# Gate and up of a feed-forward net: four sums of two products each in three shared PSUM banks, instead of two sums of five

## The chip, the cores and the metric

The kernel runs on one core of a Trainium2 chip. The metric is the device time of one execution in microseconds (us). A core has four engines that matter here: TensorE (PE in the profile; PEld are its weight loads), VectorE (DVE), ScalarE (ACT) and GpSimd (POOL). SyncE (SP) issues most DMAs. TensorE writes its results to PSUM, in banks of 512 float32 columns; VectorE and ScalarE read them from there.

## The reference

Four blocks run one after the other on x, 6250 rows of 512 numbers: a graph convolution, a feed-forward net with ternary weights, a second graph block, and a mixture of 16 experts. The change is in the feed-forward net, which the reference computes on the normalised rows:

```python
def _quantize_weight(w, group_size):            # group_size 128
    o, i = w.shape
    wg = w.reshape(o, i // group_size, group_size)
    scale = jnp.mean(jnp.abs(wg), axis=-1, keepdims=True) + EPS
    wq = jnp.clip(jnp.round(wg / scale), -1.0, 1.0) * scale
    return wq.reshape(o, i)
...
gate = _bitlinear(x, w_gate)                    # (6250, 512) by (1408, 512) transposed
up = _bitlinear(x, w_up)
h = jax.nn.silu(gate) * up
return _bitlinear(h, w_down)                    # back to 512
```

A quantised weight is -1, 0 or 1 times a scale, and there is one scale for each output feature and each block of 128 of the 512 inputs. So `gate` is a sum over four input blocks (DK = 4), each with its own scale.

## The kernel before

There are four stages, a to d. Stage a (to 168 us) makes tables for the graphs. Stage b (to about 560 us) gathers messages and prepares the weights of the feed-forward net in between. Stage c (to about 1,930 us) holds the feed-forward net, and around it the end of the first graph block and the row norms. Stage d does the rest.

**Stage b.** PE fetches table rows in 136 rounds of 20 small products (`products`, L1202 and L1205), which DVE picks out of PSUM (`pick`, L990). After every eighth round one block of 128 of the 1408 hidden features (f = 0 to 10) is prepared: ACT takes absolute values and signs, DVE quantises (`quantize`, `wide`), PE turns the blocks (`wide`, L1215 and L1216), ACT writes them to `wgu_hi`, and DVE writes a remainder to `wgu_lo` (`wide_rest`, L961). The four input blocks are taken in pairs. The even block of a pair is kept as -1, 0, 1; the odd one is multiplied by the ratio of the two scales (`wodd`, L952 to L954), so that a pair can be summed under one scale. Weights that carry this ratio are kept in a high part (`wgu_hi`) and a low part (`wgu_lo`).

**Stage c.** The 49 tiles of 128 rows are taken seven at a time, in a group of four (g = 0, 512 columns) and a group of three (g = 1, 384 columns); the seven rounds i = 0 to 6 are one unrolled, five passes of a loop, one unrolled. Each group has 11 steps, one for each f, so there are 154 steps. In a step PE does, in this order: `gate` (two sums of five products, into the banks pG0 and pG1), `up` (two sums of five, into pU0 and into pG0 again), and `down` of the step before (three products for each tile, 12 or 9, L1523). The five products of a sum are the even block's weights with the high and the low part of x, the odd block's with both, and the odd block's low part with the high part of x.

The sums leave PSUM as follows. ACT reads pG0 with the pair's scale into `gate_sum` (L1590). DVE reads pG1, scales it and adds it to `gate_sum` (L1722). ACT reads the second sum of up, which lies in pG0, into `up_sum` (L1596), and DVE adds pU0 to it (L1728). ACT makes silu of `gate_sum` in `sil` (L1599), DVE multiplies it by `up_sum` (L1732), ACT writes the high part to `hT` (L1603), DVE the low part (L1738), and `down` of the next step reads both.

**The order.** Each engine has its own queue and runs it in order. The order is written by hand in `groups`: after gate, up, low and down of each f, tables name what else is done there for the next group (`ahead`: building one-hot matrices with `build`, L173 to L1672; `sums`, L257 to L267; `layer1`, L1472, L1566 and L1680; statistics, norms, transposes) and for the last one (`behind`: residual L1744, statistics L1686, rows L1617, L1620 and L1759). This is called side work below. SP loads `wd` for each step, and POOL gathers messages (L132) beside all of it.

**Waits.** `wait_alone` makes an engine wait for a semaphore in an instruction of its own. PE may write a bank again once it has been read: gate's pG0 waits for `up_b` (ACT has read up's second sum), pG1 for `gate_b` (DVE has read it), pU0 for `up_a` (DVE), and up's pG0 for `gate_a` (ACT has read gate's first sum).

## Time and profile before

| what | value |
|---|---|
| median of 3 runs | 3246.15 us (3240.7 to 3249.64) |
| the profiled execution's own time | 3251.79 us |
| its span | 3250.0 us |
| busy in the span | PE 2693.1 us (83%), PEld 1942.7 (60%), DVE 1886.2 (58%), ACT 1259.4 (39%), POOL 1891.1 (58%) |
| mean granted clock of TensorE | 0.929 of full speed |
| steps of the feed-forward net | from 663.6 to about 1911 us |
| one pass of its loop (22 steps) | 182.34 us, from 1036.50 to 1218.84 |

The span is the time from the first to the last instruction of the profiled execution; 1.79 us of its own time lie around it. Busy shares are averages over stages with different limits, so the stages are read one by one. Durations of matmuls include their pipeline: the distance between the starts of two of them is less than the duration of one.

### The profile page before, as it was taken

The page shows a single profiled execution, that of the slowest core. Times are in us where ns is not written, and L with a number is a line of the kernel's source. Part 1 is how long each engine was busy: PE and PEld are TensorE (multiplying, and loading weights), DVE is VectorE, ACT ScalarE, POOL GpSimd, SP SyncE. Part 2 cuts the span into 40 slices and gives each one's busy share as a digit, 9 for nine tenths or more (in the row PEclk, how much of TensorE's full clock was granted, in tenths as well). Part 3 has the DMA queues.
Part 4 walks back from the last instruction along what each step waited for, and adds up shares of the span by engine and source line. Part 5 has one row for each costly group of instructions (what it writes and reads, how often), then busy time and mean ns, then how long its engine had stood idle before and what let it go on. Part 6 is the DMA issues. An engine that isn't in the chain of part 4 may idle for free. (4 is left out here: it accounts for less than half of the span.)

```text
span 3250.0 us, 59097 instructions
## 1 busy us (share of the span) xinstructions
PE 2693.1 (83%) x16318; PEld 1942.7 (60%) x16319; DVE 1886.2 (58%) x3394; ACT 1259.4 (39%) x2019; POOL 1891.1 (58%) x1940
## 2 busy tenths in 40 slices
PE   7789865579998989898999957778787887878799
PEld 7779864457777777777777743334343333435577
DVE  7679777646665565666666553333434444443687
ACT  2288643334544445444444440111222121214454
POOL 1077770577777777777400017777776767771465
PEclk9999985689999999999999978989999999998799
DMA  6354530213333333333323347777777877775574
GB/s 225 120 140 121 126 84 3 63 36 98 97 84 102 98 113 87 107 98 107 93 80 101 97 147 219 226 232 220 235 244 231 246 227 240 243 234 170 172 242 145
DMA packets 239794, 483.61 MB, mean 149 GB/s; under 512 B 75343, under 2 KB 92969, under 8 KB 239535
## 3 DMA queue, kind: packets, MB, share of 16 engines
q0 software_dynamic: 103936, 233.92, 26.6%
q1 hardware_dynamic: 135598, 246.49, 23.2%
q8 instruction: 132, 2.16, 0.3%
q14 instruction: 128, 1.04, 0.1%
HBM read 413.43 MB, written 73.35 MB: 150 GB/s over the span
## 5 line engine op out<-in xcount | busy, mean ns | idle before, releaser
L1975 POOL DMA_INDIRECT rows<-xn_rows,srcT x784 | 743.1, 948 | 273.0 <-issue 239.4
L132 POOL DMA_INDIRECT msg_c<-hid_rows,srcT x744 | 755.0, 1015 | 241.8 <-issue 225.7
L2114 PE MATMUL pV<-rows,oh 128*128 x2240 | 557.8, 398 | 145.0 <-DVE oh L2409 48.8
L1492 PE MATMUL gates<-xT,wgu_hi 128*128 128x384 f32 (+1 forms) x1848 | 481.5, 383 | 42.5 <-ACT gate_sum L1590 21.6
L2114 PEld LDWEIGHTS pV<-rows,oh 128*128 x2240 | 225.2, 101 | 463.4 <-issue 291.2
L1523 PE MATMUL accs<-wd,hT 128*128 128x512 f32 x1617 | 403.9, 397 | 15.9 <-DVE hT L1738 15.9
L1492 PEld LDWEIGHTS gates<-xT,wgu_hi 128*128 128x128 f32 x1848 | 343.1, 194 | 111.1 <-issue 65.8
L1523 PEld LDWEIGHTS accs<-wd,hT 128*128 128x128 f32 x1617 | 301.8, 188 | 87.7 <-issue 27.9
L2409 DVE SCALAR_TENSOR_TENSOR oh<-ids,bases,dstT 128x896 f32 x160 | 184.1, 1150 | 227.4 <-issue 164.0
L2397 DVE TENSOR_TENSOR agg<-agg,pV x161 | 110.1, 684 | 320.9 <-PE pV L2114 320.3
L132 POOL DMA_INDIRECT msg_b<-hid_rows,srcT x240 | 242.3, 1010 | 76.2 <-issue 72.0
L2246 ACT ACTIVATE between<-agg,invdeg 128x512 f32 (+1 forms) x49 | 35.3, 721 | 553.2 <-DVEq L121 553.2
L1205 PE MATMUL pG<-table,los 128*128 128x200 f16 x2176 | 247.5, 256 | 0.0
L1205 PEld LDWEIGHTS pG<-table,los 128*128 128x128 f16 x2176 | 200.6, 101 | 2.4
L2202 PE MATMUL pY<-weT,erT 128*128 128x512 f32 (+1 forms) x768 | 195.3, 404 | 3.8 <-DVE erT L2526 3.7
L2144 PE MATMUL pW<-wgT,aT 128*128 128x512 f32 x392 | 184.1, 614 | 15.0 <-DVEq L2432 14.9
L1958 POOL IOTA bases<- 128x49 f32 x1 | 0.2, 188 | 335.1 <-POOLq L390 335.1
L1596 ACT ACTIVATE up_sum<-gates,wscale 128x512 f32<-128x512 f32 (+1 forms) x154 | 97.6, 634 | 224.9 <-PE gates L1492 224.8
L1728 DVE SCALAR_TENSOR_TENSOR up_sum<-pU,wscale,up_sum 128x512 f32<-128x512 f32 (+1 forms) x154 | 105.0, 682 | 136.4 <-ACT up_sum L1596 132.2
L1492 PE MATMUL pU<-xT,wgu_hi 128*128 128x512 f32 (+1 forms) x616 | 168.1, 396 | 6.1 <-DVE up_sum L1728 6.1
L1492 PE MATMUL gates<-xT,wgu_lo 128*128 128x512 f32 (+1 forms) x462 | 172.3, 373 | 0.0
L1722 DVE SCALAR_TENSOR_TENSOR gate_sum<-gates,wscale,gate_sum 128x512 f32<-128x512 f32 (+1 forms) x154 | 105.3, 684 | 115.0 <-PE gates L1492 80.2
(426 smaller groups left out, 4525.0 us busy)
## 6 DMA issues: line engine op xcount, KB each, us to landing
wd<-wd_rows SPq DMA_DIRECT2D x154, 512.0 KB
lo<-lo_rows SPq DMA_DIRECT2D x68, 256.0 KB, 3.4
we<-in_L_ffn_expert_w SPq DMA_DIRECT2D x16, 1024.0 KB
x_rows<-xr SPq DMA_DIRECT2D x49, 256.0 KB, 4.3
xn_rows<-pair SPq DMA_DIRECT2D x49, 256.0 KB, 2.2
rows<-xn_rows,srcT POOLq DMA_INDIRECT x784
res<-x_rows SPq DMA_DIRECT2D x49, 256.0 KB, 3.9
x_rows<-agg SPq DMA_DIRECT2D x49, 256.0 KB, 4.1
```

The costliest lines, as they stand in the source:

```text
L132: nc.gpsimd.indirect_dma_start(msg[:, c, :], None, table, bass.IndirectOffsetOnAxis(ap=srcT[:, c:c + 1], axis=0)).then_inc(landed[u % 2], 16)
L1205: last = nc.tensor.matmul(into, los[:, g // 2 % LP, b, at:at + P], table1[:, j, b].rearrange("p f h -> p (f h)"), start=False, stop=(b == ...
L1492: last = nc.tensor.matmul(ps[:, 0:n], w, v, start=(m == 0), stop=(m == len(terms) - 1))
L1523: last = nc.tensor.matmul(acc4[j][:], h, wd[:, slot, w, :], start=(f == 0 and m == 0), stop=(f == FB - 1 and m == 2))
L1722: nc.vector.scalar_tensor_tensor(gate_sum[:, 0:n], pG[1][:, 0:n], wscale[:, f, 1:2], gate_sum[:, 0:n], ALU.mult, ALU.add).then_inc(s["gate ...
L1728: nc.vector.scalar_tensor_tensor(up_sum[:, 0:n], pU[0][:, 0:n], wscale[:, FB + f, 0:1], up_sum[:, 0:n], ALU.mult, ALU.add).then_inc(s["up_ ...
L1975: nc.gpsimd.indirect_dma_start(rows[:, u % RING, c, :], None, xn2_rows, bass.IndirectOffsetOnAxis(ap=srcT[:, u * Q + c:u * Q + c + 1], axi ...
L2114: last = nc.tensor.matmul(pV[:, ds(to, 1), :].rearrange("p a d -> p (a d)"), oh[:, ds(to, 1), c, :].rearrange("p a d -> p (a d)"), rows[:, ...
L2144: nc.tensor.matmul(pW[:], aT[:, k % 2, c, :], wgT[:, c, :], start=(c == 0), stop=False)
L2202: last = nc.tensor.matmul(pY[f % 2][0:n, :], erT[:, f % 2, j, c, 0:n], weT[:, e % 2, k, c, :], start=(j, k, c) == terms[0], stop=(j, k, c) ...
L2397: nc.vector.tensor_tensor(at, at, pV[:, ds((v + 1) % 2, 1), :].rearrange("p a b -> p (a b)"), ALU.add).then_inc(s["added"], 1)
L2409: nc.vector.scalar_tensor_tensor(oh[:, ds(v % 2, 1)].rearrange("p a q n -> p (a q) n"), bc(ids.unsqueeze(1), (P, Q, P)), bases[:, ds(tile, ...
```

## The change

A sum now takes one input block alone: its two products are the block's weights (-1, 0, 1) with the high and the low part of x. Gate has four such sums and so has up, in three banks that are used in a ring: gate's go to pG0, pG1, pU0, pG0, up's to pG1, pU0, pG0, pG1. ACT still reads the first sum of each, and DVE the other three, each scaled and added to `gate_sum` or `up_sum`, one after the other. `wgu_lo`, `wodd` and the work that made them are gone; `wscale` holds four scales for each feature, not two. The silu on ACT now waits for the third of DVE's sums, and PE's waits on a bank follow the ring.

```diff
-        wgu_lo = sb(ffn, "wgu_lo", [P, 2 * FB, DK // 2, P], F32R)
-        wscale = sb(ffn, "wscale", [P, 2 * FB, DK // 2], F32)
+        wscale = sb(ffn, "wscale", [P, 2 * FB, SP], F32)
...
-                    even, odd = (sc[:, 1, 0:2 * DK].rearrange("p (e b) -> p e b", b=2)[:, :, b] for b in range(2))
-                    ratio = sc[:, 3, 0:DK]
-                    nc.vector.tensor_copy(wscale[:].rearrange("p (k f) e -> p k f e", k=2)[:, :, f, :], even.rearrange("p (k e) -> p k e", k=2))
-                    own.step(nc.vector.reciprocal(ratio, even))
-                    own.step(nc.vector.tensor_mul(ratio, odd, ratio))
-                    nc.vector.tensor_tensor(wodd[:], wthree[:].rearrange("p (e b) c -> p e b c", b=2)[:, :, 1, :],
-                                            bc(ratio.unsqueeze(2), (P, DK, P)), ALU.mult).then_inc(s["wq"], 1)
+                    scales = sc[:, 1, 0:2 * DK].rearrange("p (k e) -> p k e", k=2)
+                    nc.vector.tensor_copy(wscale[:].rearrange("p (k f) e -> p k f e", k=2)[:, :, f, :], scales).then_inc(s["wq"], 1)
...
-                def wide_rest(f):
-                    dve.wait_ge(s["hi"], f + 1)
...
                     for j in range(2):
-                        for e in range(DK // 2):
-                            nc.tensor.matmul(pW[:, j, 2 * e, :], wthree[:, j * DK + 2 * e, :], identb[:], start=True, stop=True)
-                            last = nc.tensor.transpose(pW[:, j, 2 * e + 1, :], wodd[:, j * DK // 2 + e, :], ident[:])
+                        for e in range(SP):
+                            last = nc.tensor.matmul(pW[:, j, e, :], wthree[:, j * DK + e, :], identb[:], start=True, stop=True)
...
-            pU = [pb(ctx, "pU0", [P, 4 * P], F32), pG[0]]
+            pU = [pb(ctx, "pU0", [P, 4 * P], F32)]
+            ring = [pG[0], pG[1], pU[0]]
+            gate_at = [ring[e % 3] for e in range(SP)]
+            up_at = [ring[(SP + e) % 3] for e in range(SP)]
...
                 def hidden(ps, g, f, which, e):
-                    hi, lo = wgu_hi[:, which * FB + f], wgu_lo[:, which * FB + f]
+                    hi = wgu_hi[:, which * FB + f]
                     x_hi, x_lo = xT[g][:, 0], xT[g][:, 1]
                     n = len(GROUPS[g]) * P
-                    a, b = 2 * e, 2 * e + 1
-                    terms = ((hi[:, a, :], x_hi[:, a, :]), (hi[:, a, :], x_lo[:, a, :]), (hi[:, b, :], x_hi[:, b, :]),
-                             (hi[:, b, :], x_lo[:, b, :]), (lo[:, e, :], x_hi[:, b, :]))
+                    terms = [(hi[:, e, :], x_hi[:, e, :]), (hi[:, e, :], x_lo[:, e, :])]
...
-                    wait_alone(pe, s["up_b"], step + 1, s["fence_pe"])
-                    hidden(pG[0], g, f, 0, 0).then_inc(s["gate_ps"], 1)
-                    wait_alone(pe, s["gate_b"], step + 1, s["fence_pe"])
-                    hidden(pG[1], g, f, 0, 1).then_inc(s["gate_ps"], 1)
+                    wait_alone(pe, s["up_b"], 3 * step + 2, s["fence_pe"])
+                    hidden(gate_at[0], g, f, 0, 0).then_inc(s["gate_ps"], 1)
+                    wait_alone(pe, s["up_b"], 3 * step + 3, s["fence_pe"])
+                    hidden(gate_at[1], g, f, 0, 1).then_inc(s["gate_ps"], 1)
+                    hidden(gate_at[2], g, f, 0, 2).then_inc(s["gate_ps"], 1)
+                    wait_alone(pe, s["gate_a"], step + 1, s["fence_pe"])
+                    hidden(gate_at[3], g, f, 0, 3).then_inc(s["gate_ps"], 1)
 
                 def up(i, g, f):
                     step = steps_before(i, g, f)
-                    wait_alone(pe, s["up_a"], step + 1, s["fence_pe"])
-                    hidden(pU[0], g, f, 1, 0).then_inc(s["up_ps"], 1)
-                    wait_alone(pe, s["gate_a"], step + 1, s["fence_pe"])
-                    hidden(pU[1], g, f, 1, 1).then_inc(s["up_ps"], 1)
+                    wait_alone(pe, s["gate_b"], 3 * step + 1, s["fence_pe"])
+                    hidden(up_at[0], g, f, 1, 0).then_inc(s["up_ps"], 1)
+                    wait_alone(pe, s["gate_b"], 3 * step + 2, s["fence_pe"])
+                    hidden(up_at[1], g, f, 1, 1).then_inc(s["up_ps"], 1)
+                    wait_alone(pe, s["gate_b"], 3 * step + 3, s["fence_pe"])
+                    hidden(up_at[2], g, f, 1, 2).then_inc(s["up_ps"], 1)
+                    wait_alone(pe, s["up_a"], step + 2, s["fence_pe"])
+                    hidden(up_at[3], g, f, 1, 3).then_inc(s["up_ps"], 1)
...
-                    dve.wait_ge(s["gate_ps"], 2 * step + 2)
                     dve.wait_ge(s["gate_a"], step + 1)
-                    nc.vector.scalar_tensor_tensor(gate_sum[:, 0:n], pG[1][:, 0:n], wscale[:, f, 1:2], gate_sum[:, 0:n],
-                                                   ALU.mult, ALU.add).then_inc(s["gate_b"], 1)
+                    for e in range(1, SP):
+                        dve.wait_ge(s["gate_ps"], SP * step + (e + 1))
+                        if e > 1:
+                            dve.wait_ge(s["gate_b"], (SP - 1) * step + (e - 1))
+                        nc.vector.scalar_tensor_tensor(gate_sum[:, 0:n], gate_at[e][:, 0:n], wscale[:, f, e:e + 1], gate_sum[:, 0:n],
+                                                       ALU.mult, ALU.add).then_inc(s["gate_b"], 1)
```

`up` on DVE is changed as `gate` is, with `up_ps`, `up_b` and `up_at`; ACT's two reads take `gate_at[0]` and `up_at[0]`.

On PE, the rows of the step f = 1 of the first group of four tiles, before (gates holds two banks, pU is the third; x4 is four products in a row):

```order
L1492 MATMUL gates<-xT,wgu_hi 128x512 x4
L1492 MATMUL gates<-xT,wgu_lo 128x512
L1492 MATMUL gates<-xT,wgu_hi 128x512 x4
L1492 MATMUL gates<-xT,wgu_lo 128x512
L1492 MATMUL pU<-xT,wgu_hi 128x512 x4
L1492 MATMUL pU<-xT,wgu_lo 128x512
L1492 MATMUL gates<-xT,wgu_hi 128x512 x4
L1492 MATMUL gates<-xT,wgu_lo 128x512
L1523 MATMUL accs<-wd,hT 128x512 x12
```

and the same step in the changed kernel (line 1492 has become 1478, line 1523 has become 1516):

```order
L1478 MATMUL gates<-xT,wgu_hi 128x512 x4
L1478 MATMUL pU<-xT,wgu_hi 128x512 x2
L1478 MATMUL gates<-xT,wgu_hi 128x512 x4
L1478 MATMUL pU<-xT,wgu_hi 128x512 x2
L1478 MATMUL gates<-xT,wgu_hi 128x512 x4
L1516 MATMUL accs<-wd,hT 128x512 x12
```

The step has 16 products where it had 20, and the bank changes after every two of them (x4 in gates is two sums of two products in its two banks) where it changed after five.

On DVE, the rows of one step f = 0 and the first of the next step, before:

```order
L1722 SCALAR_TENSOR_TENSOR gate_sum<-gates,wscale,gate_sum 128x512
L1728 SCALAR_TENSOR_TENSOR up_sum<-pU,wscale,up_sum 128x512
L1732 TENSOR_TENSOR sil<-up_sum,sil 128x512
L1738 TENSOR_TENSOR hT<-sil,hT 128x512
L1722 SCALAR_TENSOR_TENSOR gate_sum<-gates,wscale,gate_sum 128x512
```

and in the changed kernel (1722 has become 1718, the other three lines happen to keep their numbers):

```order
L1718 SCALAR_TENSOR_TENSOR gate_sum<-gates,wscale,gate_sum 128x512
L1718 SCALAR_TENSOR_TENSOR gate_sum<-pU,wscale,gate_sum 128x512
L1718 SCALAR_TENSOR_TENSOR gate_sum<-gates,wscale,gate_sum 128x512
L1728 SCALAR_TENSOR_TENSOR up_sum<-pU,wscale,up_sum 128x512
L1728 SCALAR_TENSOR_TENSOR up_sum<-gates,wscale,up_sum 128x512 x2
L1732 TENSOR_TENSOR sil<-up_sum,sil 128x512
L1738 TENSOR_TENSOR hT<-sil,hT 128x512
L1718 SCALAR_TENSOR_TENSOR gate_sum<-gates,wscale,gate_sum 128x512
```

Three instructions that read PSUM stand where one stood, once for gate and once for up; the product with silu (L1732) and the low half (L1738) keep their places behind them.

On DVE in the stage that prepares the weights, the piece of one block of features before:

```order
L941 TENSOR_SCALAR sc<-sc 128x8
L942 TENSOR_TENSOR wthree<-wsize,sc 128x1024
L943 TENSOR_TENSOR wthree<-wthree,wsign 128x1024
L951 COPY wscale<-sc 128x2x2
L952 RECIPROCAL sc<-sc 128x4
L953 TENSOR_TENSOR sc<-sc 128x4
L954 TENSOR_TENSOR wodd<-wthree,sc 128x512
L990 TENSOR_REDUCE picked<-pG 128x32
```

and in the changed kernel:

```order
L940 TENSOR_SCALAR sc<-sc 128x8
L941 TENSOR_TENSOR wthree<-wsize,sc 128x1024
L942 TENSOR_TENSOR wthree<-wthree,wsign 128x1024
L949 COPY wscale<-sc 128x2x4
L977 TENSOR_REDUCE picked<-pG 128x32
```

The three rows that made wodd are gone, and so is, further down, the subtraction that wrote wgu_lo.

## Rows read from the trace of the kernel before

**Rows 1.** Stretches: us, busy and count of PE, PEld, DVE, ACT, POOL; clock; DMA.

```profile
663.60:1911.00 1247.40, 1143.82 (x6222) 931.06 (x6223) 752.05 (x1534) 580.27 (x968) 704.02 (x693) 0.97 0.33 96
1036.50:1218.84 182.34, 166.84 (x909) 135.10 (x910) 111.91 (x230) 85.01 (x142) 138.13 (x136) 0.97 0.35 97
475.00:560.00 85.00, 38.55 (x858) 31.98 (x858) 66.81 (x74) 29.01 (x78) 5.58 (x6) 0.50 0.02 3
```

**Rows 2.** Timeline of PE, one loop pass: start us, us, instruction.

```profile
1091.50 2.90 PE L1523 MATMUL accs<-wd,hT 128*128 128x512 f32 x12
1094.23 1.10 PE L1492 MATMUL gates<-xT,wgu_hi 128*128 128x512 f32 x4
1095.17 0.39 PE L1492 MATMUL gates<-xT,wgu_lo 128*128 128x512 f32 x1
...
1182.68 2.25 PE L1523 MATMUL accs<-wd,hT 128*128 128x512 f32 x9
1184.76 0.86 PE L1492 MATMUL gates<-xT,wgu_hi 128*128 128x384 f32 x4
```

**Rows 3.** Instructions of line 1492: duration ns min/median/max, first and last start.

```profile
L1492 PE MATMUL gates<-xT,wgu_lo x462: 332/388/632, 665.5 to 1906.5; 128*128 128x512 f32 x77, 128*128 128x384 f32 x77
...
L1492 PE MATMUL pU<-xT,wgu_lo x154: 332/392/525, 669.5 to 1905.6; 128*128 128x512 f32 x77, 128*128 128x384 f32 x77
```

**Rows 4.** Groups by form, DVE, 1036.5 to 1218.84: busy us, mean ns, idle before.

```profile
L1722 DVE SCALAR_TENSOR_TENSOR gate_sum<-gates,wscale,gate_sum 128x512 f32<-128x512 f32 x11 | 8.3, 751 | 14.7 <-PE gates L1492 12.3 <-ACT gate_sum L1590 1.3 <-DVE small L1692 0.6
...
L1738 DVE TENSOR_TENSOR hT<-sil,hT 128x512 fp32r<-128x512 f32 x11 | 7.6, 692 | 8.4 <-ACT hT L1603 8.4
...
L1722 DVE SCALAR_TENSOR_TENSOR gate_sum<-gates,wscale,gate_sum 128x384 f32<-128x384 f32 x11 | 6.8, 618 | 5.2 <-PE gates L1492 2.0 <-ACT gate_sum L1590 1.9 <-DVE small L1692 0.6
...
L1738 DVE TENSOR_TENSOR hT<-sil,hT 128x384 fp32r<-128x384 f32 x11 | 6.3, 569 | 7.1 <-ACT hT L1603 7.1
...
L1680 DVE SCALAR_TENSOR_TENSOR xr<-xn,small,xr 128x512 f32<-128x512 f32 x7 | 5.3, 752 | 6.1 <-ACT xn L1566 6.1
...
L1672 DVE TENSOR_SCALAR first_id<-first_id 128x1 f32<-128x1 f32 x7 | 1.1, 154 | 2.2 <-DVE onehot L183 2.2
```

**Rows 5.** Timeline of DVE, the same pass.

```profile
1092.42 0.75 DVE L1728 SCALAR_TENSOR_TENSOR up_sum<-pU,wscale,up_sum 128x512 f32<-128x512 f32 x1 [2.30 <-ACT up_sum L1596]
1093.20 0.69 DVE L1732 TENSOR_TENSOR sil<-up_sum,sil 128x512 f32<-128x512 f32 x1
...
1105.29 0.75 DVE L1722 SCALAR_TENSOR_TENSOR gate_sum<-gates,wscale,gate_sum 128x512 f32<-128x512 f32 x1 [1.31 <-ACT gate_sum L1590]
...
1223.04 0.75 DVE L1722 SCALAR_TENSOR_TENSOR gate_sum<-gates,wscale,gate_sum 128x512 f32<-128x512 f32 x1 [5.55 <-PE gates L1492]
```

**Rows 6.** Timeline of all engines, 1140 to 1143: a hand-over.

```profile
1140.59 0.62 DVE L1722 SCALAR_TENSOR_TENSOR gate_sum<-gates,wscale,gate_sum 128x384 f32<-128x384 f32 x1 [0.31 <-DVE small L1692]
...
1141.35 0.94 PE L1492 MATMUL gates<-xT,wgu_hi 128*128 128x384 f32 x4 [0.29 <-DVE gate_sum L1722]
...
1142.13 0.34 PE L1492 MATMUL gates<-xT,wgu_lo 128*128 128x384 f32 x1
```

**Rows 7.** Timeline of PE: after three waits.

```profile
1161.33 0.95 PE L1492 MATMUL gates<-xT,wgu_hi 128*128 128x384 f32 x4 [2.03 <-ACT gate_sum L1590]
...
1169.92 1.10 PE L1472 MATMUL pB<-w2b,aggT 128*128 128x512 f32 x2 [2.67 <-ACT aggT L1556]
1170.45 1.78 PE L1492 MATMUL pU<-xT,wgu_hi 128*128 128x384 f32 x4
```

**Rows 8.** Timeline of all engines, 245 to 263: weights' stage.

```profile
245.45 0.17 DVE L952 RECIPROCAL sc<-sc 128x4 f32<-128x4 f32 x1
...
245.85 0.69 DVE L954 TENSOR_TENSOR wodd<-wthree,sc 128x512 f32<-128x512 bf16 x1
...
246.60 0.23 PE L1215 MATMUL pW<-identb,wthree 128*128 128x128 bf16 x1 [0.53 <-DVE wodd L954]
...
250.59 0.67 DVE L961 TENSOR_TENSOR wgu_lo<-pW,wgu_hi 128x512 fp32r<-128x512 f32 x1
```

More of the change, by code:

```diff
@@ L43 @@
 M = 136
+SP = 4
 MB = 4
@@ L789, in program @@
         s = {n: sem("b_" + n) for n in (
-            "numbered ext_in small_in wq signs ps hi lo_done dve msg onehot used agg var std hid2 stored halves "
+            "numbered ext_in small_in wq signs ps hi dve msg onehot used agg var std hid2 stored halves "
             "tail picked d_wq d_signs d_ps d_hi d_lo d_out evens odds besides prod reduced far related staged fetched pool tables".split())}
@@ L915, in _ @@
                 sp.wait_ge(s["d_out"], DK * 32)
-                sp.wait_ge(s["lo_done"], FB)
+                sp.wait_ge(s["hi"], FB)
                 sp.wait_ge(s["hid2"], 1)
@@ L1008, in _ @@
                         kind, i = piece_at(g, back)
-                        if kind == "wide" and back == 3:
-                            wide_rest(i)
                         if kind == "down" and back == 3:
@@ L1221, in down @@
                         pe.wait_ge(s["d_wq"], i + 1)
-                        pe.wait_ge(s["lo_done"], FB)
+                        pe.wait_ge(s["hi"], FB)
                     if i > 0 or m == 2:
@@ L1421, in _ @@
             def _(pe):
-                for n in ("used", "silu", "hmul", "xT_lo", "gate_b", "up_a", "up_b"):
+                for n in ("used", "silu", "hmul", "xT_lo", "up_a"):
                     pe.sem_inc(s[n], 1)
+                pe.sem_inc(s["up_b"], SP - 1)
                 pe.sem_inc(s["down"], 2)
@@ L1588, in gate @@
                     act.wait_ge(s["silu"], step + 1)
-                    act.wait_ge(s["gate_ps"], 2 * step + 1)
-                    nc.scalar.activation(gate_sum[:, 0:n], pG[0][:, 0:n], ACT.Identity, scale=wscale[:, f, 0:1]).then_inc(s["gate_a"], 1)
+                    act.wait_ge(s["gate_ps"], SP * step + 1)
+                    nc.scalar.activation(gate_sum[:, 0:n], gate_at[0][:, 0:n], ACT.Identity, scale=wscale[:, f, 0:1]).then_inc(s["gate_a"], 1)
                 def up(i, g, f):
@@ L1594, in up @@
                     act.wait_ge(s["hmul"], step + 1)
-                    act.wait_ge(s["up_ps"], 2 * step + 2)
-                    nc.scalar.activation(up_sum[:, 0:n], pU[1][:, 0:n], ACT.Identity, scale=wscale[:, FB + f, 1:2]).then_inc(s["up_b"], 1)
+                    act.wait_ge(s["up_ps"], SP * step + 1)
+                    nc.scalar.activation(up_sum[:, 0:n], up_at[0][:, 0:n], ACT.Identity, scale=wscale[:, FB + f, 0:1]).then_inc(s["up_a"], 1)
                     act.wait_ge(s["h_lo"], step + 1)
-                    act.wait_ge(s["gate_b"], step + 2)
+                    act.wait_ge(s["gate_b"], (SP - 1) * step + (SP - 1))
                     nc.scalar.activation(sil[:, 0:n], gate_sum[:, 0:n], ACT.Silu).then_inc(s["silu"], 1)
@@ L1719, in gate @@
                     step, n = steps_before(i, g, f), len(GROUPS[g]) * P
-                    dve.wait_ge(s["gate_ps"], 2 * step + 2)
                     dve.wait_ge(s["gate_a"], step + 1)
-                    nc.vector.scalar_tensor_tensor(gate_sum[:, 0:n], pG[1][:, 0:n], wscale[:, f, 1:2], gate_sum[:, 0:n],
-                                                   ALU.mult, ALU.add).then_inc(s["gate_b"], 1)
+                    for e in range(1, SP):
[4 more added lines that the diff above has]
+                                                       ALU.mult, ALU.add).then_inc(s["gate_b"], 1)
                 def up(i, g, f):
                     step, n, slot = steps_before(i, g, f), len(GROUPS[g]) * P, (g * FB + f) % 2
-                    dve.wait_ge(s["up_b"], step + 2)
-                    nc.vector.scalar_tensor_tensor(up_sum[:, 0:n], pU[0][:, 0:n], wscale[:, FB + f, 0:1], up_sum[:, 0:n],
-                                                   ALU.mult, ALU.add).then_inc(s["up_a"], 1)
                     dve.wait_ge(s["up_a"], step + 2)
+                    for e in range(1, SP):
+                        dve.wait_ge(s["up_ps"], SP * step + (e + 1))
+                        if e > 1:
+                            dve.wait_ge(s["up_b"], (SP - 1) * step + (SP - 1 + e - 1))
+                        nc.vector.scalar_tensor_tensor(up_sum[:, 0:n], up_at[e][:, 0:n], wscale[:, FB + f, e:e + 1], up_sum[:, 0:n],
+                                                       ALU.mult, ALU.add).then_inc(s["up_b"], 1)
+                    dve.wait_ge(s["up_b"], (SP - 1) * step + 2 * (SP - 1))
                     dve.wait_ge(s["silu"], step + 2)
```

7 lines of the change are left out of this document (1 added, 6 removed).

## The prediction

> **What bounds the kernel now.** I read the stretches first, then PE's timeline in a loop pass, then the groups of DVE. The steps of the feed-forward net fill 1247.40 us, 38% of the span, with PE busy for 1143.82 us of it and DVE for 752.05 [rows 1]. One loop pass of 22 steps takes 182.34 us, so the stretch holds 6.84 such passes. In PE's timeline the matmuls stand back to back: twelve products of `down`, then at once the next gate [rows 2]. From the rows, products of 512 columns follow each other every (1.10 - 0.39) / 3 = 0.237 us, those of `down` every (2.90 - 0.39) / 11 = 0.228, those of 384 columns every (0.86 - 0.34) / 3 = 0.173 [rows 2, 6]. PE is the bound there. DVE is busy for 111.91 of the 182.34 us [rows 1], and much of its idle time ends with PE: 12.3 us before L1722 in eleven steps of 512 columns [rows 4]. It waits for PE, and PE seldom for it.
>
> **What goes.** The removed products are the 462 and 154 of `wgu_lo` [rows 3], 616, four in a step, half of them of 512 columns: 308 x 0.237 + 308 x 0.173 = 126 us of PE, 18.0 us a pass. If PE stayed the bound this would be the gain.
>
> In stage b one prepared block loses on DVE three instructions, from 245.45 to 245.85 + 0.69 = 246.54, and PE's transposes, which wait for them, start at 246.60 after 0.53 us of waiting [rows 8]; the subtraction of 0.67 us goes as well. PE gains its wait and about half a microsecond of what DVE held up behind it, 1.0 us in eleven blocks: 11 us. Lower bound nothing, where the gather hides it; upper bound 1.1 + 0.67 = 1.8 us a block, 20 us.
>
> **What comes: DVE.** Every step gets four more DVE instructions that read PSUM, of the kind of L1722: 0.751 us at 512 columns and 0.618 at 384 [rows 4]. That is 44 x 0.751 + 44 x 0.618 = 60.2 us a pass, and DVE's 111.9 become 172.1 of a pass that now takes 182.3. This alone would still fit. What doesn't fit is the idle time that DVE can't fill:
>
> - 8.4 + 7.1 = 15.5 us before L1738, where it waits for ACT's high part of the same step [rows 4]. This wait stays as it is.
> - 0.03 us between two dependent instructions: 1092.42 + 0.75 to 1093.20 [rows 5]. Four new ones a step: 2.6 us.
> - Short gaps inside its own side work, the largest 2.2 us before L1672 [rows 4]; with the other small lines I take 7.
> - Waits for ACT in `layer1`, 6.1 us before L1680 [rows 4]. DVE comes later there, so I take half, 3.
> - At the end of a pass DVE waits 5.55 us while PE starts the loop again [rows 5]. The first sum now has two products, not ten ahead of DVE: I take 3.
> - ACT's norms and transposes stand ahead of its read of gate's first sum: 1.31 us at 1105.29 [rows 5], in two steps of each group; four times 1.3 is 5.
> - The hand-over of a bank. In [rows 6] DVE ends at 1140.59 + 0.62 = 1141.21 and the five products behind its semaphore at 1142.13 + 0.34 = 1142.47, 1.26 us later; two products take 3 x 0.173 less, 0.74 us. DVE's next read hides 0.65 of it, so up's first read by DVE waits about 0.1 us a step: 2.
> - Steps without side work. PE can run only three sums ahead of DVE: gate's fourth needs ACT's read, up's first DVE's first. From the end of gate's last read PE has to do: the hand-over (five products from release 1.26, alone 4 x 0.173 + 0.34 = 1.03, so 0.23), four products of up, `down`, gate's first sum (0.237 + 0.39), ACT's read (taken as long as DVE's, 0.75), and DVE's three reads again: 0.23 + 0.95 + 2.74 + 0.63 + 0.75 + 2.34 = 7.64 us at 512 columns. DVE's own chain, six reads, L1732, the wait, L1738, is 6 x 0.78 + 0.72 + 0.76 + 0.72 + 0.1 = 6.98. In about four such steps of each group the difference (0.66, and 0.3 at 384) is lost on DVE: 4.
>
> Together 42 us, and 172.1 + 42 = 214 us a pass against 182.3: +32. PE's 18 saved microseconds don't appear, since PE now waits.
>
> Side work was free for PE before, since it needed DVE only once a step for each bank. Now a block of DVE work, such as building a one-hot or statistics, lies in the only chain. That cover is gone in most steps, and with it goes PE's.
>
> **The clock.** After idle times PE can be slow: after 2.67 us of waiting, four products of 384 columns took 1.78 us instead of 0.86, after 2.03 us they took 0.95 [rows 2, 7]. Where PE was busy for only 38.55 of 85 us, the granted clock was 0.50, its 1.2 GHz level [rows 1]. In the changed stage I count 12 of 22 steps whose side work on DVE, 2.5 us or more, leaves PE without work for over 2 us. At half speed a hand-over takes about twice 0.74, 0.65 us more than DVE's next read hides, once a step: 12 x 0.65 x 6.84 = 53 us. As not every such wait lowered the clock, I take 50; the bounds are 0 and, with every step slow, 98. The Trainium skill ("TensorE: Matmul & The Clock Gate", section "Why this matters for your kernels") says to avoid idle gaps between bursts of matmuls, as they bring the lower clock back; by this rule it would be the whole 53. The 2.03 us above are a case where this trace does not show it.
>
> **The sum**, against the profiled execution's own 3251.8 us: 32 x 6.84 = 219; less 16, as the first group has no side work behind it and the last none ahead (a fourteenth of the growth); plus 50 for the clock; less 11 in stage b. +242 us, 3494. That execution was 5.6 us above the median of the runs shown, so 3488.
>
> **The rivals.**
>
> *PE stays the bound (faster).* The evacuation hides behind the matmuls and the 126 + 11 us are gained: 3251.8 - 137 = 3115, 3109 as a median. It would need DVE to be done in 182.3 - 18 = 164 us a pass. With 111.9 + 15.5 us that stay, its 88 new reads could take 0.42 us each; [rows 4] have 0.62 and 0.75. Nothing in the trace speaks for so short a read. The Trainium skill ("Perfetto Trace Analysis", section "Matmuls") advises to rotate independent sums through different PSUM banks, so that the evacuation of one overlaps the matmuls of the next; this is what the ring does, and by that rule it would be this rival. It decides only while the engine that empties the banks has time left. 3 in 100.
>
> *DVE bound, but nearly packed.* Only the first three items of idle time stay (25 us), the clock holds: 197 us a pass, +15 x 6.84 - 8 - 11 = +84, 3336; with half of the other terms about 3380. For it: DVE's queue moves side work into waits that now seem lost. Against it: DVE's waits for ACT and PE in one step are in a chain, with nothing to put between. 14 in 100.
>
> *Worse chain.* Idle terms half as large again and most steps at the lower clock: +53 x 6.84 = 363 - 20 + 98 - 11 gives 3680; its lower edge is 3610. For it: the stretch at 0.50. 15 in 100.
>
> *It makes no difference* (gain and loss cancel within 0.3%, 10 us; about what a measurement of this kernel can tell from no change): 3246. It needs a pass of 184 us, thus 12 us of idle time on DVE, less than the 15.5 of L1738 alone. 2 in 100. A loss that is smaller than 3380 otherwise: 2 in 100.
>
> **How the numbers follow.** My forecast, 3380 to 3610 around 3488, has 64 in 100; the range reaches to 3380 and 3620 and takes in the upper edge of the packed case and the lower edge of the worse one. Faster 0.04 (the first rival and a little more), same 0.02, slower 0.94.
>
> **What would show it.** In the profile after: the 616 products gone and no `wgu_lo`; 616 more DVE reads of PSUM at 0.62 and 0.75 us; in the stretch of the steps DVE busy for 752 + 616 x 0.685 = 1174 us, about four fifths of it; a pass of about 214 us plus 7 for the clock; PE's waits ended by DVE at L1718 and L1728 among the longest (before they hardly show), DVE's wait for ACT before L1738 the same 0.70 us a step; a granted clock in the stretch of 0.8 to 0.9 instead of 0.97; one prepared block in stage b a microsecond shorter; stages a and d unchanged. Wrong would be: DVE reads that overlap and take less than their durations, a pass near 190, or PE's waits ending at ACT rather than DVE.

## The result, and the profile after

The changed kernel took 3498.9 us (median of 4 runs, 3493.85 to 3501.08); the kernel before, run beside it, 3243.43 (3236.25 to 3249.64). The ratio is 1.0786, with a 95% interval of 1.076 to 1.0813: 255 us more, where 242 were forecast. The profiled execution of the changed kernel took 3501.08 us, 249.3 more than that of the kernel before.

The first part of the page shows TensorE's busy time hardly higher (2693.1 us before) and VectorE's 405 us higher (1886.2 before).

```profile
PE 2749.3 (79%) x15702; PEld 1853.8 (53%) x15703; DVE 2291.0 (65%) x3966; ACT 1262.4 (36%) x2019; POOL 1899.1 (54%) x1940
```

The stretches come next, with the columns of [rows 1]: the steps of the net, and one loop pass from the first read of gate to the same read a pass later.

```profile
647.30:2166.40 1519.10, 1215.77 (x5611) 849.15 (x5611) 1172.21 (x2151) 583.56 (x968) 699.40 (x694) 0.90 0.28 78
1095.16:1314.87 219.71, 174.94 (x819) 123.00 (x819) 172.06 (x319) 85.12 (x142) 166.38 (x165) 0.89 0.30 82
```

The stretch grew from 1247.40 to 1519.10 us, +271.7. It began 16.3 us earlier, and what follows it took 6.1 us less: 271.7 - 16.3 - 6.1 = 249.3, all of the growth. TensorE is busy for 72 us more, although 616 products are gone; VectorE for 1172.21 us in place of 752.05. In the pass VectorE is busy for 172.06 of 219.71 us.

Line 1478 is now `hidden`: its matmuls (duration in ns, first and last start) name `wgu_hi` alone, with the same counts as before.

```profile
L1478 PE MATMUL gates<-xT,wgu_hi x1848: 331/397/799, 647.3 to 2160.7; 128*128 128x512 f32 x93, 128*128 128x384 f32 x92
...
L1478 PE MATMUL pU<-xT,wgu_hi x616: 331/393/767, 649.2 to 2159.6; 128*128 128x512 f32 x77, 128*128 128x384 f32 x77
```

The groups of VectorE by form in that pass answer to [rows 4]; L1718 reads gate's sums, L1728 up's.

```profile
L1718 DVE SCALAR_TENSOR_TENSOR gate_sum<-gates,wscale,gate_sum 128x512 f32<-128x512 f32 x23 | 17.3, 751 | 11.8 <-PE pU L1478 4.1 <-PE gates L1478 4.1 <-ACT gate_sum L1583 2.5
...
L1728 DVE SCALAR_TENSOR_TENSOR up_sum<-gates,wscale,up_sum 128x384 f32<-128x384 f32 x22 | 13.6, 618 | 0.8
...
L1728 DVE SCALAR_TENSOR_TENSOR up_sum<-pU,wscale,up_sum 128x512 f32<-128x512 f32 x11 | 8.2, 750 | 2.0 <-PE pU L1478 0.9 <-ACT up_sum L1589 0.5 <-DVE small L1691 0.3
L1738 DVE TENSOR_TENSOR hT<-sil,hT 128x512 fp32r<-128x512 f32 x11 | 7.6, 694 | 8.7 <-ACT hT L1596 8.7
```

A new read takes what an old one took, 751 and 618 ns. The wait before L1738 is about what it was, 8.7 us in eleven steps. What VectorE loses otherwise lies before gate's reads (L1718; the group holds the first and the third of a step), little before up's.

The waits in the stretch (us in total, times, longest):

```profile
ACT hT L1596 <- DVE sil L1732: 403.8, 153, 4.4
ACT up_sum L1589 <- PE gates L1478: 301.8, 115, 14.2
...
PE gates L1478 <- DVE gate_sum L1718: 193.1, 105, 12.1
DVE hT L1738 <- ACT hT L1596: 109.5, 153, 1.1
```

The third line is the new one: 105 times TensorE stands, nearly always before up's first sum, until VectorE has read gate's second; 57 of these waits are longer than 2 us. In the timeline of a step that follows side work it looks like this:

```profile
1105.97 0.17 DVE L1685 TENSOR_SCALAR small<-small 128x3 f32<-128x3 f32 x1
...
1106.38 0.75 DVE L1718 SCALAR_TENSOR_TENSOR gate_sum<-gates,wscale,gate_sum 128x512 f32<-128x512 f32 x1 [0.24 <-DVE small L1685]
...
1107.28 1.19 PE L1478 MATMUL gates<-xT,wgu_hi 128*128 128x512 f32 x2 [2.79 <-DVE gate_sum L1718]
...
1109.44 0.75 DVE L1728 SCALAR_TENSOR_TENSOR up_sum<-pU,wscale,up_sum 128x512 f32<-128x512 f32 x1 [0.73 <-PE pU L1478]
```

VectorE was at statistics until 1106.14; TensorE waited 2.79 us, its next two products took 1.19 us (0.61 to 0.70 in the step of the next excerpt), and VectorE then waited 0.73 us for up. A step with little side work shows the other side, in the timeline of VectorE:

```profile
1139.77 0.75 DVE L1718 SCALAR_TENSOR_TENSOR gate_sum<-gates,wscale,gate_sum 128x512 f32<-128x512 f32 x1 [0.24 <-ACT gate_sum L1583]
...
1141.34 0.75 DVE L1718 SCALAR_TENSOR_TENSOR gate_sum<-gates,wscale,gate_sum 128x512 f32<-128x512 f32 x1
1142.01 0.68 DVE L1759 TENSOR_TENSOR pair<-xn,pair 128x512 f16<-128x512 f32 x1
...
1146.41 0.69 DVE L1738 TENSOR_TENSOR hT<-sil,hT 128x512 fp32r<-128x512 f32 x1 [0.76 <-ACT hT L1596]
1147.48 0.75 DVE L1718 SCALAR_TENSOR_TENSOR gate_sum<-gates,wscale,gate_sum 128x512 f32<-128x512 f32 x1 [0.38 <-ACT gate_sum L1583]
```

Here VectorE had 0.68 us of side work to do and still waited 0.38 us at the next gate: not its own work ended the step but TensorE's and ScalarE's. In the last steps of the stretch, which have no side work, one step is 6.25 us long (timeline of all engines):

```profile
2145.35 0.62 DVE L1718 SCALAR_TENSOR_TENSOR gate_sum<-gates,wscale,gate_sum 128x384 f32<-128x384 f32 x1 [0.21 <-PE pU L1478]
...
2146.79 0.62 DVE L1718 SCALAR_TENSOR_TENSOR gate_sum<-gates,wscale,gate_sum 128x384 f32<-128x384 f32 x1
...
2147.56 0.94 PE L1478 MATMUL gates<-xT,wgu_hi 128*128 128x384 f32 x4
...
2148.33 2.21 PE L1516 MATMUL accs<-wd,hT 128*128 128x512 f32 x9
...
2150.38 0.86 PE L1478 MATMUL gates<-xT,wgu_hi 128*128 128x384 f32 x4
...
2150.83 0.56 DVE L1738 TENSOR_TENSOR hT<-sil,hT 128x384 fp32r<-128x384 f32 x1 [0.65 <-ACT hT L1596]
...
2150.99 0.58 ACT L1583 ACTIVATE gate_sum<-gates,wscale 128x384 f32<-128x384 f32 x1 [0.26 <-PE gates L1478]
...
2151.60 0.62 DVE L1718 SCALAR_TENSOR_TENSOR gate_sum<-gates,wscale,gate_sum 128x384 f32<-128x384 f32 x1 [0.21 <-PE pU L1478]
```

From gate's last read (2146.79) TensorE does two sums of up, `down`, and gate's first sum, ScalarE reads that (to 2151.57), and VectorE can go on at 2151.60 (the row names `pU`, the modelled end of the sum after it; ScalarE's end is the nearer). VectorE's own chain ended at 2150.83 + 0.56 = 2151.39, 0.21 us earlier. In this step there are two chains, and they are almost equally long.

### The profile page after: what moved, and what is told of

It reads as the page before. It is cut to its first block and busy times, and to the rows that moved or that the text cites. A ratio compares the mean times of both kernels' runs of the same rounds, so it can differ in the third digit from the quotient of the medians.

```text
span 3499.2 us, 60360 instructions
## 1 busy us (share of the span) xinstructions
PE 2749.3 (79%) x15702; PEld 1853.8 (53%) x15703; DVE 2291.0 (65%) x3966; ACT 1262.4 (36%) x2019; POOL 1899.1 (54%) x1940
## 5 line engine op out<-in xcount | busy, mean ns | idle before, releaser
L1478 PE MATMUL gates<-xT,wgu_hi 128*128 128x384 f32 (+1 forms) x1848 | 598.2, 433 | 273.1 <-DVE gate_sum L1718 193.1
L1516 PE MATMUL accs<-wd,hT 128*128 128x512 f32 x1617 | 442.0, 424 | 14.1 <-DVE hT L1738 14.1
L1516 PEld LDWEIGHTS accs<-wd,hT 128*128 128x128 f32 x1617 | 335.2, 210 | 98.6 <-issue 25.8
L133 POOL DMA_INDIRECT msg_b<-hid_rows,srcT x240 | 254.8, 1062 | 76.1 <-issue 73.4
L1718 DVE SCALAR_TENSOR_TENSOR gate_sum<-gates,wscale,gate_sum 128x512 f32<-128x512 f32 (+1 forms) x308 | 210.7, 684 | 86.5 <-ACT gate_sum L1583 37.8
L1596 ACT CAST hT<-sil 128x512 fp32r<-128x512 f32 (+1 forms) x154 | 87.3, 567 | 406.4 <-DVE sil L1732 403.8
L1728 DVE SCALAR_TENSOR_TENSOR up_sum<-gates,wscale,up_sum 128x512 f32<-128x512 f32 (+1 forms) x308 | 210.8, 684 | 18.9 <-PE gates L1478 0.2
L1478 PE MATMUL pU<-xT,wgu_hi 128*128 128x512 f32 (+1 forms) x616 | 205.7, 418 | 8.0 <-DVE gate_sum L1718 1.5
```

The costliest lines, as they stand in the source:

```text
L133: nc.gpsimd.indirect_dma_start(msg[:, c, :], None, table, bass.IndirectOffsetOnAxis(ap=srcT[:, c:c + 1], axis=0)).then_inc(landed[u % 2], 16)
L1478: last = nc.tensor.matmul(ps[:, 0:n], w, v, start=(m == 0), stop=(m == len(terms) - 1))
L1516: last = nc.tensor.matmul(acc4[j][:], h, wd[:, slot, w, :], start=(f == 0 and m == 0), stop=(f == FB - 1 and m == 2))
L1718: nc.vector.scalar_tensor_tensor(gate_sum[:, 0:n], gate_at[e][:, 0:n], wscale[:, f, e:e + 1], gate_sum[:, 0:n], ALU.mult, ALU.add).then_in ...
L1728: nc.vector.scalar_tensor_tensor(up_sum[:, 0:n], up_at[e][:, 0:n], wscale[:, FB + f, e:e + 1], up_sum[:, 0:n], ALU.mult, ALU.add).then_inc ...
```

## The experiments

Each kernel ran beside the kernel before; ratios are to that. Passes are measured from gate's first read to the same read a pass later.

**Shorter reads.** In VectorE's reads, two of every three:

```diff
-    ...(gate_sum[:, 0:n], gate_at[e][:, 0:n], ...
+    m = n if e == 1 else 64
+    ...(gate_sum[:, 0:m], gate_at[e][:, 0:m], ...      # up alike
```

> The changed kernel, in which VectorE's reads of the third and fourth sum of gate and of up take 64 columns in place of 512 or 384 (left out: the rest of those sums); every product, bank, semaphore and wait is as in the changed kernel. Theory (the length of VectorE's reads sets the pace): from 0.751 us at 512 columns and 0.618 at 384 a read of 64 comes to about 0.29 us, 88 reads a pass save 35 us of 220.4, and the pass comes near 184 us: 3230 to 3290 us, PE's waits much shorter. Rival (each bank costs a hand-over and a lowered clock however long its read is): the pass keeps most of its 220 us, over 3400 us. Rival (TensorE has become slower in itself, by its products of two): no change, 3499 us.

Measured: 3382.79 us, ratio 1.0444 (1.041 to 1.0478). One pass, and the groups of up's reads:

```profile
1062.41:1268.60 206.19, 168.62 (x821) 124.11 (x821) 136.81 (x319) 85.27 (x142) 157.39 (x156) 0.91 0.32 87
```
```profile
L1730 DVE SCALAR_TENSOR_TENSOR up_sum<-pU,wscale,up_sum 128x512 f32<-128x512 f32 (+1 forms) x154 | 105.1, 682 | 77.1 <-ACT up_sum L1589 56.1 <-PE pU L1478 11.0 <-PE gates L1478 7.2
...
L1730 DVE SCALAR_TENSOR_TENSOR up_sum<-gates,wscale,up_sum 128x64 f32<-128x64 f32 x308 | 87.4, 284 | 28.0 <-PE gates L1478 12.1
```

All three expectations missed. VectorE is busy for 35 us a pass less, as worked out, but the pass is only 13.5 us shorter; over the whole execution 116 us of 245 come back. The length of the reads matters, and VectorE's time alone isn't the pace: what it saves becomes waits, here for ScalarE's read of up (77.1 us before up's first read, 24.6 in the changed kernel).

**Eight products without the extra reads.** In the kernel before:

```diff
-    ... (hi[:, b, :], x_lo[:, b, :]), (lo[:, e, :], x_hi[:, b, :]))
+    ... (hi[:, b, :], x_lo[:, b, :]))
```

> The kernel before, with its two sums a matrix and its two reads, in which the fifth product of each sum is left out (left out: the low part of the odd block's weights), so eight products a matrix, as in the changed kernel. Theory (TensorE was the bound, its products were worth their time, and only the reads spoil it): 616 products of 0.237 and 0.173 us go, 126 us, so 3110 to 3135 us, and a loop pass of about 164 us. Rival (TensorE's products were hidden by something else even before, so that their removal is worth little): 3180 us or more.

Measured: 3180.75 us, ratio 0.9821 (0.9791 to 0.9852), 61 us less than the kernel before where 126 were expected. A pass:

```profile
1014.20:1184.75 170.55, 151.33 (x826) 118.94 (x826) 111.79 (x231) 84.73 (x142) 129.96 (x129) 0.96 0.37 104
```

It is 11.3 us shorter than the same pass before (181.82 us, TensorE busy for 166.32), not 18.0: TensorE's busy time falls by 15.0 us and its idle time rises by 3.7. In the stretch its waits for ScalarE's read of gate double, from the first row (the kernel before) to the second (this kernel):

```profile
PE gates L1492 <- ACT gate_sum L1590: 21.6, 25, 2.0
```
```profile
PE gates L1492 <- ACT gate_sum L1590: 43.8, 44, 2.2
```

So the product count was worth half its price by the medians and 11.3 of 18.0 us by the pass: TensorE was the bound of the kernel before with a small margin. The 318 us between this kernel and the changed one come with the four sums and their six reads.

**Ten products in the four sums.**

```diff
+    if e in (1, 2):
+        nc.tensor.matmul(ps[:, 0:n], hi[:, e, :], x_hi[:, e, :], start=True, stop=True)
```

> The changed kernel, in which the second and third sum of gate and of up begin with one more product, a repetition of their first, so that 616 products come back and TensorE has its ten a matrix again; the sums and the reads are unchanged. Theory (VectorE's chain is the bound, TensorE waits for it): most of the 126 us of products disappear in TensorE's waits, +10 to +50 us, 3510 to 3550 us. Rival (TensorE's throughput, at its granted clock, still sets the time): +126 us or more, 3625 us.

Measured: 3526.66 us, ratio 1.0881 (1.0849 to 1.0913): +28 us for 616 products that would take 126 us. As the theory said, TensorE's throughput isn't the bound; three quarters vanish in its waits.

**The low part later.** VectorE's wait of 0.7 us a step for ScalarE's cast is given something to do (ScalarE's cast moves with it):

```diff
     part.gate(i, g, f)
+    if f > 0:
+        part.low(i, g, f - 1)       # DVE: low part; ACT: cast
     beside(f, 0)
     part.up(i, g, f)
     beside(f, 0.5)
-    part.low(i, g, f)
     beside(f, 1)
...
+part.low(i, g, FB - 1)
 part.down(i, g, FB - 1)
```

> The changed kernel, in which VectorE takes the low part of the hidden row block (the instruction that waits 0.7 us a step for ScalarE's cast) behind its three reads of the next gate, and ScalarE its cast behind its read of the next gate's first sum; nothing is added or left out. Theory (VectorE's idle times lie in the chain that sets the pace, so one of them that is filled comes back): of 15.8 us a pass and 110 us in all, 80 to 110 come back, 3390 to 3420 us. Rival (VectorE's idle time moves elsewhere, since TensorE's hand-over or ScalarE's read ends just behind it): 3470 to 3500 us.

Measured: 3488.23 us, ratio 1.0761 (1.0727 to 1.0794), 11 us less than the changed kernel, inside the rival's range. But the waits showed a fault of the edit: the last low part of a group now stood behind the building of a one-hot, and TensorE's last products of the group waited for it.

```profile
PE accs L1518 <- DVE hT L1743: 65.2, 14, 5.7
```

**The low part in time**, with the last one of a group at its old place:

```diff
+    if f == FB - 1:
+        part.low(i, g, f)
     beside(f, 1)
```

> As the run with the low part taken later, but in the last step of a group the low part keeps its old place: there TensorE's last products of a group waited for it behind the building of a one-hot, 65 us in 14 waits. Theory now (two chains are nearly equal: VectorE's own, and the round from TensorE's sums through ScalarE's read and VectorE's three reads of gate back to TensorE; filling VectorE's wait shortens only the first, so it pays in the steps with side work alone): those 65 us and little more come back, 3420 to 3450 us. Rival (VectorE's time alone sets the pace): 3390 us or less. Rival (nothing of it lies on the path): 3480 us or more.

Measured: 3438.9 us, ratio 1.0595 (1.0576 to 1.0615): 60 us less than the changed kernel, as the theory of two chains had it.

**A shorter round of TensorE**, one product of `down` in three:

```diff
-    for m, (h, w) in enumerate(((h_hi, 0), (h_hi, 1), (h_lo, 0))):
-        last = nc.tensor.matmul(acc4[j][:], h, wd[:, slot, w, :], ...)
+    last = nc.tensor.matmul(acc4[j][:], h_hi, wd[:, slot, 0, :], ...)
```

> The changed kernel, in which of the three products of each row block of the second matrix only the first is left (left out: the low parts there), four and three products a step in place of twelve and nine: TensorE's round is 1.83 and 1.37 us a step shorter, VectorE's work is the same. Theory (two chains nearly equal): only what the round takes over VectorE's own chain comes back, 0.66 us in plain steps of 512 columns and 0.3 in those of 384, with the waits at gate's first read (86 us in all) as the upper bound: 3420 to 3480 us. Rival (TensorE's round sets the pace in every step): 154 times 1.6 us, 245 us less, 3255 us. Rival (VectorE's chain alone sets it): 3490 to 3500 us.

Measured: 3476.13 us, ratio 1.0709 (1.0686 to 1.0733): 23 us less than the changed kernel, although 1078 products went.

**Both.**

> Both edits together: the low part behind the next gate's reads (in a group's last step at its old place) and one product in three of the second matrix (left out: the low parts there). Theory (two chains nearly equal): with both shorter the gain is larger than the sum of the two alone, as neither is held by the other: 3300 to 3370 us. Rival (one chain sets the pace): the gain is that of the better of the two alone, within 15 us.

Measured: 3329.12 us, ratio 1.0265 (1.0244 to 1.0285): 170 us less than the changed kernel, where the two edits alone gave 60 and 23. That is the decisive run. The groups of VectorE before gate's first read (with the third) and before the low part, over the whole execution, first in the changed kernel, then with the low part in time, with the short `down`, and with both:

```profile
L1718 DVE SCALAR_TENSOR_TENSOR gate_sum<-gates,wscale,gate_sum 128x512 f32<-128x512 f32 (+1 forms) x308 | 210.7, 684 | 86.5 <-ACT gate_sum L1583 37.8 <-PE pU L1478 25.3 <-DVE small L1685 6.3
...
L1738 DVE TENSOR_TENSOR hT<-sil,hT 128x512 fp32r<-128x512 f32 (+1 forms) x154 | 96.6, 628 | 110.1 <-ACT hT L1596 109.5 <-DVE sil L1732 0.7
```
```profile
L1724 DVE SCALAR_TENSOR_TENSOR gate_sum<-gates,wscale,gate_sum 128x512 f32<-128x512 f32 (+1 forms) x308 | 210.5, 683 | 129.6 <-PE pU L1481 52.5 <-ACT gate_sum L1586 49.8 <-DVE small L1691 6.1
...
L1744 DVE TENSOR_TENSOR hT<-sil,hT 128x512 fp32r<-128x512 f32 (+1 forms) x154 | 95.2, 618 | 9.8 <-ACT hT L1602 9.8
```
```profile
L1716 DVE SCALAR_TENSOR_TENSOR gate_sum<-gates,wscale,gate_sum 128x512 f32<-128x512 f32 (+1 forms) x308 | 210.3, 683 | 59.4 <-ACT gate_sum L1581 21.9 <-PE gates L1478 14.2 <-DVE small L1683 6.3
...
L1736 DVE TENSOR_TENSOR hT<-sil,hT 128x512 fp32r<-128x512 f32 (+1 forms) x154 | 96.5, 627 | 110.3 <-ACT hT L1594 110.3
```
```profile
L1722 DVE SCALAR_TENSOR_TENSOR gate_sum<-gates,wscale,gate_sum 128x512 f32<-128x512 f32 (+1 forms) x308 | 210.3, 683 | 63.8 <-PE gates L1481 15.7 <-ACT gate_sum L1584 14.7 <-PE pU L1481 13.6
...
L1742 DVE TENSOR_TENSOR hT<-sil,hT 128x512 fp32r<-128x512 f32 (+1 forms) x154 | 95.2, 618 | 9.8 <-ACT hT L1600 9.8
```

Filling the wait for the cast frees 100 us, and 43 of them come back before gate, where the sums and ScalarE's read aren't ready. With a short `down` they are ready (63.8 us there, 59.4 with the short `down` alone), and a pass comes down to 194.82 us. The rest of the 170 us is VectorE's too: its waits before up fall from 24.6 to 6.9 us, in `layer1` from 26.6 to 12.7 and before `pair` from 14.0 to 2.1, those before `mstage` and `own_rows` rise by 22 together, and from gate's first read to its last the same 2138 instructions keep it busy for 1144.82 us in place of 1166.10, as they overlap more. A pass:

```profile
1052.83:1247.65 194.82, 138.50 (x666) 91.11 (x666) 168.99 (x318) 85.84 (x142) 148.02 (x149) 0.89 0.34 92
```

**TensorE's clock**, in two forms: products that fill TensorE's wait, in six steps of a group and then in four.

```diff
     wait_alone(pe, s["gate_a"], step + 1, s["fence_pe"])
+    if f in (0, 1, 2, 3, 4, 7):      # then (2, 3, 4, 7)
+        for _ in range(8 if g == 0 else 11):
+            nc.tensor.matmul(gate_at[3][:, 0:n], wgu_hi[:, f, 3, :], xT[g][:, 0, 3, :], start=True, stop=True)
     hidden(gate_at[3], g, f, 0, 3)
```

> The changed kernel, in which gate's fourth sum of the steps f = 0, 1, 2, 3, 4 and 7 (behind long side work of VectorE) begins with 8 more products at 512 columns or 11 at 384, repetitions that the sum then overwrites: about 1.9 us of work for TensorE in a time in which it would wait for VectorE. Nothing is left out. Theory (the clock's term is real: TensorE's matmuls behind a long wait run at half speed, and the hand-over behind them is on the path): products of gate and up that ran slow lost about 124 us in the changed kernel's stretch against 40 in the kernel before; of the difference a quarter to two thirds lies on the path, so 20 to 60 us come back, 3440 to 3480 us. Rival (slow products are hidden behind VectorE's reads): no change within 10 us, or a little slower, since the filling products end too late.

Measured: 3516.55 us, ratio 1.0849 (1.0822 to 1.0875): 18 us more than the changed kernel, where 20 to 60 less were expected.

> The changed kernel with the filling products in the steps f = 2, 3, 4 and 7 alone, where VectorE's side work is long enough to hide all of them; the run with six such steps lengthened the first two steps of a group by 1.3 us or more and won up to 1.9 us in others. Theory (the clock behind a long wait lies on the path): 8 to 25 us less than the changed kernel, 3474 to 3491 us. Rival (slow products are hidden behind VectorE's reads): 3495 to 3505 us.

Measured: 3508.38 us, ratio 1.0813 (1.0795 to 1.0831): not faster, and 3 us above the rival's range. The first six of the seven rounds, from gate's first read to gate's first read, in the changed kernel and then with the four fillings:

```profile
651.20:1972.48 1321.28, 1051.71 (x4925) 736.30 (x4926) 1022.92 (x1889) 506.83 (x844) 696.41 (x691) 0.89 0.28 78
```
```profile
657.31:1978.95 1321.64, 1102.15 (x5381) 782.38 (x5382) 1021.79 (x1889) 504.39 (x844) 699.79 (x691) 0.94 0.28 78
```

The granted clock rose from 0.89 to 0.94, and the time stayed: 1321.28 and 1321.64 us (the 9 us in the medians lie mostly ahead: the steps of this execution began 6.1 us later). The waits before up's first read, in which the clock's price was to lie, are 24.6 us in the changed kernel and 24.7 with the filling. The filling has a price too (VectorE waits for the late fourth sum, 24.7 us before gate that ended with TensorE's `gates`, 18.5 of them in these six rounds), and in the same rounds the waits before gate that ended with ScalarE's read or with `pU` fell from 52.6 to 41.3 us. So a small gain may be covered by the price; a gain of 50 us isn't there.

**Two sums without any low part of these weights**, in stage b too:

```diff
-    wide_rest(i)                       # and the waits on it; the products as above
```

> The kernel before with eight products a matrix in its two sums, and without the low parts of these weights in stage b as well (left out: the low part of the odd block's weights, in the products and in their making). Theory: the run with eight products in two sums gave 3181 us; in stage b the subtraction of 0.67 us a prepared block goes, and TensorE's wait for it: 5 to 15 us less, 3165 to 3178 us. Rival (the gather hides it): 3176 to 3186 us.

Measured: 3182.82 us, ratio 0.9819 (0.9801 to 0.9837), as with the products alone, so the rival held: the subtraction of 0.67 us in [rows 8] was hidden.

**And with the low part in time** (the edits above together):

> That kernel (two sums, eight products, no low parts of these weights), in which VectorE takes the low part of the hidden rows behind its read of the next gate, in a group's last step at its old place. Theory (with eight products TensorE has lost its lead, and the round through ScalarE and VectorE sets part of the pace, since only 61 of 126 us came back): VectorE's waits for the cast, 108 us, are filled, and 15 to 50 us come back, 3120 to 3160 us. Rival (TensorE alone is the bound): no change within 10 us.

Measured: 3169.97 us, ratio 0.9785 (0.9769 to 0.9802), the fastest kernel here. The gain of 13 us lies between the rival (within 10) and the 15 to 50 that were expected.

**The low part in time in the kernel before, whole.**

> The kernel before, whole, with VectorE's low part of the hidden rows behind its read of the next gate (in a group's last step at its old place), which gave 60 us in the changed kernel. Theory (before the change TensorE is the bound and VectorE's waits are free): no change within 15 us, 3228 to 3250 us. Rival (the wait for the cast lay on the path before too): 30 to 60 us less.

Measured: 3239.61 us, ratio 0.9991 (0.9978 to 1.0005): no change, although the wait for the cast was filled (108.3 us before the low part in the kernel before). What it set free came back as waiting for TensorE's sums, 200.0 us before gate in place of 115.0:

```profile
L1728 DVE SCALAR_TENSOR_TENSOR gate_sum<-gates,wscale,gate_sum 128x512 f32<-128x512 f32 (+1 forms) x154 | 105.3, 684 | 200.0 <-PE gates L1495 183.0 <-DVE small L1698 6.1 <-DVE first_id L1678 5.7
...
L1744 DVE TENSOR_TENSOR hT<-sil,hT 128x512 fp32r<-128x512 f32 (+1 forms) x154 | 95.1, 617 | 9.8 <-ACT hT L1609 9.8
```

The same edit is worth 60 us in the changed kernel and nothing before. A wait of 108 us on VectorE was free as long as TensorE was the bound.

## Why the prediction was right, and where it wasn't

The forecast was 3488 us, the measurement 3498.9, and the direction came from the step that mattered: VectorE's added reads don't fit beside waits that it can't fill. By its own steps:

- **What goes.** The 616 products are gone. That they would have been worth 126 us with TensorE as the bound was wrong: without the added reads they gave 61. The price of the first rival, 3109, was thus too low by 65 us; its direction wasn't touched.
- **VectorE's work.** 1174 us were forecast in the stretch, 1172.21 measured; 172.1 in a pass, 172.06 measured.
- **Idle time that VectorE can't fill**, 42 us a pass and 7 for the clock: 47.65 measured in the pass above. Item by item: the cast, 15.5 forecast, 110.1 us measured in 154 steps, 15.7 for each 22; the loop's end, 3 forecast, 4.09 and 4.07 us; `layer1`, 3 forecast, 26.6 us in all, 3.8 a pass; the three items before gate's first read (loop's end, norms, plain steps), 12 forecast or 82 us in the stretch, 86.5 measured.
- **Steps without side work.** By TensorE's round 7.64 us at 512 columns were forecast, and at 384 a round 0.3 us longer than VectorE's own chain. Measured are 7.71 us with 0.68 us of side work in it, and at 384 a step of 6.25 us in which VectorE's chain ended 0.21 us early. The prediction took this round as a term of 4 us, in four steps of a group. It reaches further: of the 100 us that the filled wait set free, 43 came back before gate, and only 4 with the short `down` (59.4 to 63.8). The sentence that a block of side work lies "in the only chain" was the step that failed: there is a second chain, through TensorE's round. It cost the sum little, since in the changed kernel the second sticks out by only some 23 us (the short `down` alone).
- **The clock**, +50: mis-sized. It fell as forecast (0.90 in the stretch), and single hand-overs took longer. But the waits of over 2 us that it priced were counted too high, 12 in 22 steps; TensorE has 57 of them for gate's reads, 8 in 22. (The price of one was put too low by the prediction's own figures: twice 0.74 less the 0.65 that is hidden is 0.83 us, not 0.65.) And the place where it was to lie, together with 14 us for the hand-over of a bank, is VectorE's wait before up's first read, which is 24.6 us in all. Raising the clock again gave nothing that can be seen. The trace agrees with the page that the prediction named (the Trainium skill, "TensorE: Matmul & The Clock Gate", section "Why this matters for your kernels") in that idle gaps came with a lower clock, 0.97 before and 0.90 after; the page ties this to the length of a gap, which the prediction left out, and the price "by this rule" was the prediction's own. The runs don't show that price: by the waits before up and by the filling, most of the loss lay beside VectorE's reads.
- **The edges**, -16: less than half of it. From gate's first read to that of the next group, the first group grew by 12.6 us and the groups between by 16 to 22, some 20 on average; but the last ten steps grew from 56.05 to 75.46, as much as the others. The last group has no work ahead, but its steps carry the work behind, and TensorE's round is longer than the 5.61 us that a step took before.
- **Stage b**, -11: -16.3 in the profiled pair. Gate's first read on VectorE begins at 652.6 us as a mean over nine executions of kernels built on the change (650.1 to 657.3), and at 666.0 over three that make the low parts (663.7 to 668.3): 13 us. Two that leave out only the subtraction are at 661.3 and 669.0, which points to the three instructions ahead of the transposes. These now start 0.34 us behind the last of VectorE's and wait for nothing:

```profile
253.87 0.17 DVE L949 COPY wscale<-sc 128x8 f32<-128x8 f32 x1
...
254.38 0.61 PE L1200 MATMUL pW<-identb,wthree 128*128 128x128 bf16 x8
```

- **The whole.** In the stretch VectorE's idle time is 1519.1 - 1172.2 = 346.9 us; the forecast's terms make 1247.4 + 219 - 16 + 50 - 1174 = 326. Of the 64 for the clock and the hand-over 24.6 came, and most of the edges' 16 didn't come off. In their place the gaps inside VectorE's side work were 67 us and not 48, and those between dependent instructions 33 and not 18, as the forecast counted the new ones alone. The errors cancelled in part, so the median being near says less than the terms do.
- **The rivals.** "TensorE stays the bound" and "no difference" are excluded by the result; "nearly packed" (3336; 3330 with the 5.6 us to the median, which weren't taken off there) by the passes of 220 us; "worse chain" (3680) by the time and by idle times near the items, 47.65 us a pass. The named signs held: TensorE's waits end with VectorE at L1718 (193.1 us; at L1728, named beside it, only 15.0), those with ScalarE's `gate_sum` are few (33.3 us), and the reads kept their 618 and 751 ns.

What stays open: how much of the clock's price the filling hid, some 20 us by the wait before up, with a part in the waits before gate that the runs don't separate; and whether the 60 us of the low part come from VectorE's instruction or from ScalarE's cast, since the edit moves both.

## What to carry to other kernels

Before work is moved from a bound engine to one with idle time, ask for each idle stretch of the second whether anything could be put there: 112 busy of 182 us looked like room for 60 more, and wasn't. Where engines hand a step round in a ring, work out both rounds, the busy engine's own queue and the path back through the others; when they are nearly equal, shortening one shows little (60 and 23 us), and both together much (170). And a wait that costs nothing under one bound is worth filling under another: the same reordering gave 0 before the change and 60 us after it.
